# A four-layer graph kernel on one core: the loop over turns written out, wait thresholds as constants, repeated waits dropped

## The reference

```python
x = _layernorm(x + _L0_gnn_ref(x, adj, ...))   # attn = tanh(A * (Xc Xp^T)) per head (8 heads of 32), out = relu(attn Xp)
x = _layernorm(x + _L1_gnn_ref(x, adj, ...))   # hypergraph conv, relu, layer norm, hypergraph conv, + x
x = _layernorm(x + _L2_gnn_ref(x, adj, ...))   # row-normalised A * exp(leaky_relu(..)), X Wk0 + T X Wk1 + T T X Wk2, relu
x = _layernorm(x + _L3_gnn_ref(x, adj, ...))   # gated x, sigmoid QK, scores * adj normalised, out Wl + xg Wr, relu
```

## Time and profile before

| | us |
|---|---|
| median of 3 runs | 1863.97 |
| lowest and highest run | 1861.16 and 1866.59 |
| the profiled execution | 1869.18 |
| its span, first to last instruction | 1867.4 |
| PE, PEld, DVE, ACT, POOL busy | 1804.8, 1580.2, 1564.4, 1222.0, 871.8 |

### The profile page before, as it was taken

One profiled execution on the slowest core, in us unless ns is written; L12 is line 12 of the kernel. 1 busy time (PEld: TensorE's weight loads), 2 busy tenths in 40 slices (PEclk: granted clock), 3 DMA queues, 4 the chain that ended last, 5 costly groups with the idle time before them and its releaser, 6 DMA issues. The chain is left out here.

```text
span 1867.4 us, 50850 instructions
## 1 busy us (share of the span) xinstructions
PE 1804.8 (97%) x14472; PEld 1580.2 (85%) x14472; DVE 1564.4 (84%) x4444; ACT 1222.0 (65%) x2384; POOL 871.8 (47%) x1807
## 2 busy tenths in 40 slices
PE   5799999999999999999999999999999999999985
PEld 4678888888888888888888888888888888888874
DVE  4678888888888888888888888888888888888874
ACT  3556666676676676676676666667667667667653
POOL 1335445444544544544544544544454454454443
PEclk9899999999999999999999999999999999999998
DMA  4111112112112112112111111211211211211101
GB/s 152 38 41 58 35 58 62 42 51 62 47 45 62 48 45 62 55 37 62 62 31 62 62 34 59 62 42 51 62 48 45 62 48 45 62 55 37 40 29 34
DMA packets 99487, 97.68 MB, mean 52 GB/s; under 512 B 8320, under 2 KB 90368, under 8 KB 99200
## 3 DMA queue, kind: packets, MB, share of 16 engines
q1 hardware_dynamic: 99456, 97.29, 16.7%
HBM read 80.48 MB, written 16.78 MB: 52 GB/s over the span
## 5 line engine op out<-in xcount | busy, mean ns | idle before, releaser
L419 ACT ACTIVATE x<-res,shift,rstd 128x256 f32<-128x256 f32 x512 | 278.5, 594 | 84.8 <-DVE res L900 65.6
L405 POOL TENSOR_SCALAR edge_m<-edge_n 128x2 f32<-128x2 f32 x64 | 14.2, 222 | 483.1 <-issue 470.3
L615 DVE BATCH_NORM_STATS2 stats<-res 128x6 f32<-128x256 f32 x512 | 191.7, 416 | 0.3
L980 PE MATMUL psum<-wk_hi,xT_hi 128*128 128x258 f32 (+1 forms) x512 | 185.9, 363 | 3.4 <-DVE xT_lo L610 3.4
L319 POOL TENSOR_TENSOR rstd<-var_eps,minus_half 128x2 f32<-128x2 f32 x256 | 178.1, 696 | 20.1
L347 POOL TENSOR_TENSOR x_rest<-x,b_half 128x512 f32<-128x512 f32 x64 | 81.7, 1277 | 221.3 <-DVE res L661 221.3
L980 PE MATMUL psum<-wk_hi,xT_lo 128*128 128x258 f32 (+1 forms) x512 | 173.7, 339 | 0.0
L631 DVE TENSOR_TENSOR masked<-psum,adjT 128x512 f32<-128x512 f32 x256 | 163.9, 683 | 11.3 <-PE psum L1043 3.4
L980 PE MATMUL psum<-wk_lo,xT_hi 128*128 128x258 f32 (+1 forms) x512 | 173.0, 338 | 0.0
L578 ACT ACTIVATE z<-hid_relu,hid_bias,hid_rstd 128x512 f32<-128x512 f32 x128 | 97.5, 808 | 107.3 <-POOL hid_bias L384 107.3
L980 PE MATMUL psum<-w_hi,zT_hi 128*128 128x256 f32 x512 | 144.3, 282 | 2.3 <-DVE zT_lo L610 1.2
(11 more groups left out here) (180 smaller groups left out, 6009.4 us busy)
## 6 DMA issues: line engine op xcount, KB each, us to landing
adjT<-in_adj_t SPq DMA_DIRECT2D x256, 128.0 KB, 2.2
xt_in<-in_xt SPq DMA_DIRECT2D x64, 256.0 KB, 2.9
x<-in_x SPq DMA_DIRECT2D x64, 256.0 KB, 2.7
out<-x SPq DMA_DIRECT2D x64, 256.0 KB, 2.3
wts<-in_adj SPq DMA_DIRECT2D x64, 128.0 KB, 2.2
wts<-in_w SPq DMA_DIRECT2D x1, 1028.0 KB, 7.4
wts<-in_w SPq DMA_DIRECT2D x1, 1024.0 KB, 12.2
wts<-in_w SPq DMA_DIRECT2D x1, 769.0 KB, 9.4
```

The costliest lines, as they stand in the source:

```text
L405: pool.tensor_scalar(edge_m[:, :], edge_n[:, :], 1.0, 1.0, ALU.max, ALU.mult).then_inc(sem("edge_0"), 1)
L419: last = act.activation(xs[k + 1][:, g, :], res[k][:, g, :], ACT.Identity, scale=rstd[k][:, g:g + 1], bias=shift[k][:, g:g + 1])
L615: last = dve.bn_stats(stats[k][:, g, :], res[k][:, g, :])
L980: last = pe.matmul(dst, a, r, start=b == 0 and j == 0, stop=b == len(lhs) - 1 and j == 2)
```

## The change

All 71 turns are written out by Python, on every engine; there is no loop, no loop register and no branch. Every threshold is a constant, so `Count` and the `snap` arithmetic go. `wait` keeps, per engine and semaphore, the highest value waited for so far (`met`) and leaves out a wait whose value is not above it. `claim` waits for the one tenant that holds the bank, in all turns (`holder`), after the waits passed in `also`, which are no longer merged with it. The `sem_inc` instructions that only carried waits go. The order of the work on each engine, the tiles, the DMAs and the banks stay as they are.

```diff
-                if key not in turn.values:
-                    turn.values[key] = turn.eng.snap(turn.i * unit + key[1])
-                return turn.values[key]
...
+        met = {}
+
         def wait(eng, name, count, unit=1):
+
             less = 0
             whole, part = part_of(name)
             if part is not None:
                 unit = PARTS[whole]
                 less = unit - 1 - part
-            value = count.times(unit, less)
-            if value is not None:
+            value = unit * count - less
+            if count > 0 and value > met.get((eng, whole), 0):
+                met[eng, whole] = value
                 eng.wait_ge(sem(name), value)
 
         def turns(eng, turn):
-            for i in range(STAGES - 1):
-                turn(eng, Turn(eng, i))
-            if PAIRS > STAGES - 1:
-                with eng.Fori(STAGES - 1, PAIRS) as i:
-                    turn(eng, Turn(eng, i))
-            for i in range(max(PAIRS, STAGES - 1), TURNS):
+            for i in range(TURNS):
                 turn(eng, Turn(eng, i))
...
-            def await_on_sp(name, count, unit=1):
-                wait(sp, name, count, unit)
-                sp.sem_inc(sem("sp_waits"), 1)
...
-                    pool.sem_inc(sem("pool_waits"), 1)
...
-                dve.sem_inc(sem("dve_waits"), 1)
...
-            taken, claims = [], [0] * len(TENANTS)
...
+            holder = [None] * BANKS
 
             def claim(names, t, *also):
 
-                found = {}
                 for signal, count in also:
-                    whole, part = part_of(signal)
-                    found[whole, count] = part or 0, signal
+                    wait(pe, signal, count)
                 for name in names.split():
-                    if t.static and BANK[TENANT[name]] in taken:
+                    _, bank, stage, emptied = TENANTS[TENANT[name]]
+                    if holder[bank] == "beta":
                         pe.wait_ge(sem("beta_w2"), 1)
-                    for signal, count in waits_of(name, t):
-                        whole, part = part_of(signal)
-                        found[whole, count] = max(found.get((whole, count), (0, "")), (part or 0, signal))
-                for (_, count), (_, signal) in found.items():
-                    wait(pe, signal, count)
+                    elif holder[bank]:
+                        wait(pe, *holder[bank])
+                    holder[bank] = emptied, t.n[stage]
```

More of the change, by code:

```diff
@@ L201, in value @@
             return t.bitcast(F32)
[L203 to L213, removed]
-                if key not in turn.values:
-                    turn.values[key] = turn.eng.snap(turn.i * unit + key[1])
-                return turn.values[key]
         class Turn:
             def __init__(self, eng, i):
-                self.eng, self.i, self.values = eng, i, {}
-                self.static = isinstance(i, int)
-                counts = [Count(self, 1 - k) for k in range(STAGES + 1)]
+                self.i = i
+                counts = [min(max(i + 1 - k, 0), PAIRS) for k in range(STAGES + 1)]
                 self.n, self.p = counts[:-1], counts[1:]
-                self.on = [not self.static or 0 <= i - k < PAIRS for k in range(STAGES)]
+                self.on = [0 <= i - k < PAIRS for k in range(STAGES)]
             def first(self, k):
-                return self.static and self.i == k
+                return self.i == k
+        met = {}
         def wait(eng, name, count, unit=1):
@@ L261, in turn @@
                 if on[1]:
-                    await_on_sp("inc", p[1])
-                    await_on_sp("edge_w", p[1])
+                    wait(sp, "inc", p[1])
+                    wait(sp, "edge_w", p[1])
                     sp.dma_start(adjT[1][:, :, :].rearrange("p g n -> p (g n)"),
@@ L268, in turn @@
                         sp.wait_ge(sem("w1_lo"), 1)
-                    await_on_sp("deg", p[5])
+                    wait(sp, "deg", p[5])
                     sp.dma_start(adj_n[:, :, :], pair_at(adj, (t.i - 5) * (G * P * P))).then_inc(sem("adj_n_loaded"), 16)
                 if on[1]:
-                    await_on_sp("res0", p[1])
+                    wait(sp, "res0", p[1])
                     sp.dma_start(xs[0][:, :, :], pair_at(x, (t.i - 1) * (G * P * D))).then_inc(sem("x0_loaded"), 16)
                 if on[0]:
-                    await_on_sp("xT0_hi", p[0])
-                    await_on_sp("xT0_lo", p[0])
+                    wait(sp, "xT0_hi", p[0])
+                    wait(sp, "xT0_lo", p[0])
                     sp.dma_start(xt_in[:, :, :, :].rearrange("p c g n -> p (c g n)"),
@@ L284, in turn @@
                 if on[5]:
-                    await_on_sp("alpha", p[5])
+                    wait(sp, "alpha", p[5])
                     sp.dma_start(adjT[2][:, :, :].rearrange("p g n -> p (g n)"),
                                  rows_at(adj_t, (t.i - 5) * (G * P * P))).then_inc(sem("adj2_loaded"), 16)
-                    await_on_sp("scores", p[5])
+                    wait(sp, "scores", p[5])
                     sp.dma_start(adjT[3][:, :, :].rearrange("p g n -> p (g n)"),
@@ L294, in turn @@
                 if on[0]:
-                    await_on_sp("masked_3", p[0])
+                    wait(sp, "masked_3", p[0])
                     sp.dma_start(adjT[0][:, :, :].rearrange("p g n -> p (g n)"),
@@ L298, in turn @@
                 if on[7]:
-                    await_on_sp("x4", n[7])
+                    wait(sp, "x4", n[7])
                     sp.dma_start(pair_at(out, (t.i - 7) * (G * P * D)), xs[4][:, :, :]).then_inc(sem("stored"), 16)
@@ L941, in _ @@
         def _(pe):
-            taken, claims = [], [0] * len(TENANTS)
[L944 to L953, removed]
+            holder = [None] * BANKS
             def claim(names, t, *also):
-                found = {}
                 for signal, count in also:
-                    whole, part = part_of(signal)
-                    found[whole, count] = part or 0, signal
+                    wait(pe, signal, count)
                 for name in names.split():
-                    if t.static and BANK[TENANT[name]] in taken:
+                    _, bank, stage, emptied = TENANTS[TENANT[name]]
+                    if holder[bank] == "beta":
                         pe.wait_ge(sem("beta_w2"), 1)
-                    for signal, count in waits_of(name, t):
-                        whole, part = part_of(signal)
-                        found[whole, count] = max(found.get((whole, count), (0, "")), (part or 0, signal))
-                for (_, count), (_, signal) in found.items():
-                    wait(pe, signal, count)
+                    elif holder[bank]:
+                        wait(pe, *holder[bank])
+                    holder[bank] = emptied, t.n[stage]
             def claim_once(name, t):
[L972 to L975, removed]
+                bank = BANK[TENANT[name]]
+                if holder[bank]:
+                    wait(pe, *holder[bank])
+                holder[bank] = "beta"
             def split_product(dst, lhs, rhs, name=None):
```

1 line of the change is left out of this document (removed).

## The result

The changed kernel takes 1860.62 us (median of 20 runs, 1857.28 to 1869.03), the kernel before 1864.54 (20 runs, 1860.88 to 1870.81): ratio 0.9975, interval 0.9965 to 0.9985. The forecast was 1864.0, no change. The time lies within the range given and within 0.3% of before, but the difference is measured, and the forecast had none. The sum was built from two terms that nearly cancel, and both came out near the size worked out. What it lacked was a third: the level of PE's clock in the ramp (the turns in which the eight stages fill) and the drain (those in which they empty).

What follows compares the result with a forecast made beforehand. PE was taken to bound the steady part. Steady turns and loop's end +1.2 us, drain waits -1.2 us, sum 0 against the profiled 1869.18 us; carried to the median, 1864.0 us, range 1855 to 1870 (own range 1860 to 1867).

Steps and rivals of the forecast that it cites:

- two terms that nearly cancel: Steady turns with the passage at the loop's end, +1.2 us, against shorter waits in the drain, -1.2 us.
- The branch's gap passes to the mask: Turn's wrap on PE: without the branch, `pxT` waits for DVE's mask instead, +0.02 us per turn; chance 0.65.
- the rival with the 3.76 us passage: Scores' start to `pxT`'s end takes 3.76 us, -0.07 per turn, with the drain 1858.8 us; chance 0.12.
- The steady turn, 27.74: A turn goes from 27.72 to 27.74 us, +1.1 us over 57 turns.
- the 0.32 us: PE's loss per turn at the wrap; if wholly won, 18 us faster, 1844.5 us; chance 0.06.
- another live wait: Slower rival: the masks' 0.10 us delay makes a later wait, as before `hop2`, bind; +5.7 us, 1869.7; chance 0.08.
- Fetches: Straight-line code needs some 112 more instruction blocks on PE; costed at nothing; rival that they show, chance 0.09.
- The rival at 1898: Fetches show: a quarter of a fetch, 0.3 us, unhidden at each of 112 blocks, +34 us; chance 0.09.
- Waits in the drain, -1.2: Single bank claims and no repeated waits win 1.2 us of PE weight loader idle time in the drain.
- The six rows: Weight loader idle times in the last 130 us, between 0.4 and 0.2 us each, 1.5 us together.
- The ramp: Idle time there is mostly waits for first data and weights, so no gain was counted in the sum.
- The limit of 5.6 us: Smallest difference a measurement of this kernel was taken to tell, about 0.3%.

Runs made afterwards that it cites:

- the live wait first: Changed kernel with DVE's masks waiting for the scores first and PE waiting for `pxT`'s bank first: 1854.29 us, ratio 0.9944.
- the masks moved: Scores moved ahead of `prop`, first two masks ahead of the edge work: kernel before 1865.48 us, ratio 0.9998; changed kernel 1852.54 us, ratio 0.9927.
- the 144 products: Unread PE products added in ramp and drain: kernel before 1853.92 us, ratio 0.9935; changed kernel 1853.53 us, ratio 0.9933.

## Why the prediction was wrong, point by point

- *The branch's gap passes to the mask*: right. Rows gone, masks 1.29 us behind the scores with an idle 0.36 us (0.35 said), 0.36 us before `pxT` (0.30 said), passage 3.85. One detail was off: 0.24 us stay before `hop1_1`, which waits for the first mask. The runs with the live wait first and with the masks moved show the mechanism by undoing it. The time alone wouldn't: 1860.62 lies in the forecast's own range and also in that of the rival with the 3.76 us passage, 1856 to 1861; the passage and the turn decide.
- *The steady turn, 27.74*: 27.73 over the last 55 turns, +1.0 us in the profiled pair for the +1.1 said. The kernel before varies as much between its own traces (27.72 and 27.73, and 27.70 with the 144 products), so the size isn't shown, only that no gain of the 0.32 us is there, and no 0.1 us of another live wait.
- *Fetches*: 116 blocks for some 128, with PE 1500.00 of 1500 us busy between 200 and 1700 us; nothing. The rival at 1898 is out.
- *Waits in the drain, -1.2*: the size is right, in part by luck. The six rows from which it was taken, 1.5 us put to "issue", are four rows and 1.2 us in the changed kernel: 0.3 us. The gain lies elsewhere, in waits put to other engines. PE's idle stretches between the products of the drain are, nearly all, shorter by 0.02 to 0.38 us each, 1.1 us net between the two profiled executions. The largest gain stands before a `hop1` of the drain: 1.02 us idle in the kernel before, at 1832.78, and now

```profile
1822.63 1.13 PE L997 MATMUL psum<-y,alpha 128*128 128x257 f32 x4 [0.65 <-DVE alpha L810]
```

- *The ramp*: the failed step. The prediction gave its waits 0 to 1.5 us, took 0 (they measured 1.0) and went on, since the ramp's idle time "is mostly waits for first data and weights". It never asked at which level PE runs between those waits, though the kernel before shows a clock of 0.50 at 66 to 72 us. In the pair of traces, passes at the lower level make most of the 8.8 us: 7.1 us of busy time, of which the eight L1092 products alone are 1.73 us, 3.62 - 1.89. The sum had no term for it, and its range took only what instructions could add or remove. The limit of 5.6 us below which it saw no difference was too wide as well: twenty runs of each tell 0.1%.
- What the measured 3.9 us (4.7 by the ratio) is made of, then: about 0 from the work itself (0.4 us with PE kept at work), the rest from how often and how long PE is at its lower level, in ramp and drain. That this differs from run to run is shown by the kernel before itself, 4.2 us in the ramp of two executions. On which part of the change the gain hangs is shown too: without the memory of waits it is gone (ratio 1.0002). Why the dropped repeats bring a better level in the mean of the runs stays open: shorter waits leave PE idle for less and may let the level rise sooner, but no run separates that.

The Trainium skill's page "TensorE: Matmul & The Clock Gate", section "HAM oscillation — how this bites in real kernels", describes products that wait for data, after which the next start at the lower level. The trace of the kernel before agrees in two places: ahead of the passes at clock 0.50, at 66 us and again at 91, PE had waited twice, for 1.55 and 1.56 us. But the same two waits, 1.55 and 1.50 us, stand in the changed kernel's trace ahead of 85.21 us, and there the passes keep the higher level. So such waits need not bring the fall. The second wait and the pass behind it, before and then after:

```profile
66.85 0.80 PE L980 MATMUL psum<-w_hi,pxT_hi 128*128 128x512 f32 x1 [1.56 <-DVE pxT_lo L610]
...
85.21 0.50 PE L942 MATMUL psum<-w_hi,pxT_hi 128*128 128x512 f32 x1 [1.50 <-DVE pxT_lo L588]
```

## What to carry to other kernels

A gap that goes is only won if nothing else was just in time behind it; look for who starts within 0.1 us of the gap's end, and move that first. Of several waits before one instruction, write the one that will be live first: here it was worth 0.16 us a turn, more than the whole removal of the loop. Before comparing two kernels to a quarter of a per cent, look at PE's level in ramp and drain by the times of equal products, and keep PE at work there: by the ratios it gave some 12 us to the kernel before and 8 to the changed one, and its runs lay within about 2 us, where those of the kernel before beside them spread over 7.5. And leave out waits that are met already: with the loop written out, the whole gain of the change hung on that.

## What the runs showed of the hardware that was not expected

- Products that nobody reads make the kernel faster: 144 of them, ratio 0.9935, since the useful ones then run at PE's higher level.
- The clock column reads 1.00 from 36 to 46 us of the kernel before, while the eight products from 41.55 on take 3.62 us in place of 1.89.
- Waits that are met already are not free on PE: behind a live one they come 0.105 us apart, and at `mix_0` they held the product back by 0.16 us a turn. In ramp and drain the repeated ones cost some 2 us of PE's idle time.
